# Cross-attention and a quantised feed-forward on one core: biases spread by TensorE, weight pieces loaded in series, shorter fillings

## The reference

```
x = x + xattn(layernorm(x), ctx, ctx)
    q, k, v = Wq x + bq, Wk ctx + bk, Wv ctx + bv      # 64 x 64, over the axis of 64
    per head h of 8 (64 columns): softmax(q_h k_h^T / 8) v_h ; then Wo . + bo
x = x + (silu(n @ G) * (n @ U)) @ W   with n = layernorm(x), G, U: 512 x 1792, W: 1792 x 512
    G = (gate_w - gate_z) * gate_s   per group of 128 rows, U and W likewise
```

## Time and profile before

| | |
|---|---|
| runs | 442.44, 443.42, 445.05 us; median 443.42 |
| the profiled execution | 441.19 us, of it 439.4 in the span of the instructions |
| first gate/up product | 51.65 us after the start of the span |
| busy | TensorE 94%, VectorE 75%, ScalarE 76%, GpSimd 62% |

### The profile page before, as it was taken

How to read it: one execution, slowest core, us unless ns; L and a number is a source line. 1 busy time by engine, 2 the same in 40 slices (tenths; PEclk the granted TensorE clock), 3 DMA queues, 4 the chain that set the end, 5 groups by cost and what they waited for, 6 DMA issues and landing times.

```text
span 439.4 us, 10920 instructions
## 1 busy us (share of the span) xinstructions
PE 414.5 (94%) x4318; PEld 325.2 (74%) x4318; DVE 328.9 (75%) x576; ACT 332.0 (76%) x542; POOL 270.6 (62%) x269
## 2 busy tenths in 40 slices
PE   7598898999997999999999999999999999999994
PEld 6476756777764777777877777687877888888872
DVE  4866647899779876879787876978887667677676
ACT  2236799889766978777868878777978998988970
POOL 4444696999597656655746656654666555555561
PEclk9989999999999999999999999999999999999999
DMA  7996261976652000000210000000010000001003
GB/s 195 362 326 199 75 207 57 331 244 217 207 185 66 25 1 27 1 27 0 75 51 24 1 1 25 3 25 25 0 50 2 0 2 0 24 25 48 2 1 95
DMA packets 26917, 35.52 MB, mean 81 GB/s; under 512 B 1962, under 2 KB 18514, under 8 KB 26866
## 3 DMA queue, kind: packets, MB, share of 16 engines
q1 hardware_dynamic: 26354, 34.69, 24.1%
q0 software_dynamic: 192, 0.07, 0.4%
q10 hardware_dynamic: 320, 0.07, 0.1%
HBM read 30.63 MB, written 4.19 MB: 79 GB/s over the span
## 4 chain that ended last, share of the span: by engine, by line
PE 72%; DVE 8%; issue 8%; ACT 6%; POOL 3%; DMA 1%; SPq 1%; POOLq 0%; DVEq 0%; ACTq 0%
PE banks L754 20%; PE banks L756 18%; PE banks L767 10%; PE banks L768 9%; PE banks L652 3%; ACT banks L554 2%; DVE yT L989 2%; PE banks L692 2%; PE banks L681 2%; PE banks L670 2%; PE banks L785 2%; PE banks L662 2%; DMA x_sb<-in_x 1%; DVE st L878 1%; POOL wgu_in L410 1%
## 5 line engine op out<-in xcount | busy, mean ns | idle before, releaser
L554 ACT ACTIVATE banks<-banks,ratio 128x512 f32<-128x512 f32 x336 | 208.0, 665 | 35.2 <-PE banks L756 25.6
L989 DVE SCALAR_TENSOR_TENSOR yT<-banks,sd,yT 128x512 f32<-128x512 f32 x208 | 154.1, 747 | 48.7 <-PE banks L768 48.1
L754 PE MATMUL banks<-xT,wgu 128*128 128x512 f32 x448 | 182.5, 407 | 4.7 <-DVE t_sb L974 3.4
L756 PE MATMUL banks<-xT,wgu 128*128 128x512 f32 x448 | 175.1, 391 | 0.0
L417 POOL TENSOR_TENSOR t_sb<-t_sb,u_sb 128x512 f32<-128x512 f32 x56 | 72.7, 1298 | 64.9 <-DVE t_sb L974 64.7
L754 PEld LDWEIGHTS banks<-xT,wgu 128*128 128x128 f32 x448 | 84.1, 188 | 27.5 <-issue 3.5
L756 PEld LDWEIGHTS banks<-xT,wgu 128*128 128x128 f32 x448 | 84.3, 188 | 15.1
L767 PE MATMUL banks<-hr,wd 128*128 128x512 f32 x224 | 89.3, 399 | 4.5 <-DVE yT L989 2.7
L768 PE MATMUL banks<-hr,wd 128*128 128x512 f32 x224 | 87.5, 391 | 0.0
L430 POOL TENSOR_TENSOR hr<-t_sb,hr 128x512 fp32r<-128x512 f32 x56 | 72.6, 1297 | 5.1 <-ACT hr L576 0.7
L767 PEld LDWEIGHTS banks<-hr,wd 128*128 128x128 f32 x224 | 42.0, 188 | 19.6 <-DVE yT L989 9.9
(11 more groups left out here) (88 smaller groups left out, 398.3 us busy)
## 6 DMA issues: line engine op xcount, KB each, us to landing
x_sb<-in_x SPq DMA_DIRECT2D x16, 256.0 KB, 5.7
out<-x_sb SPq DMA_DIRECT2D x16, 256.0 KB, 2.1
wgu_in<-in_L_ffn_gate_w SPq DMA_DIRECT2D x7, 512.0 KB, 8.1
z_in<-in_L_ffn_gate_z SPq DMA_DIRECT2D x7, 512.0 KB, 5.1
wgu_in<-in_L_ffn_up_w SPq DMA_DIRECT2D x7, 512.0 KB, 5.5
z_in<-in_L_ffn_up_z SPq DMA_DIRECT2D x7, 512.0 KB, 5.1
wd_in<-in_L_ffn_down_w SPq DMA_DIRECT2D x7, 512.0 KB, 5.5
z_in<-in_L_ffn_down_z SPq DMA_DIRECT2D x7, 512.0 KB, 4.7
```

The lines of the kernel that those rows point to most:

```text
L554: act.activation(banks[:, bank, :], banks[:, bank, :], ACT.Copy, scale=ratio[:, m, g, it:it + 1]).then_inc(done[n % 2], 1)
L754: pe.matmul(banks[:, bank, :], w, xT[:, c % 2, 0, g, :], start=g == 0, stop=False, skip_group_check=True)
L756: pe.matmul(banks[:, bank, :], w, xT[:, c % 2, 1, g, :], start=False, stop=True, skip_group_check=True).then_inc(full[n % 2], 1)
L989: dve.scalar_tensor_tensor(y, bank, sd[:, it, b:b + 1], y, ALU.mult, ALU.add).then_inc(s_free, 1)
```

## The change

Five edits. (1) bq, bk, bv and bo are loaded as rows of one partition; TensorE spreads them by products with a row of ones (bq and bk over 128 partitions in one product, bv and bo into columns by four), and VectorE copies the results to `bqk` and `bvo`. TensorE waits for bq and bk ahead of `project(0)`. The waits for `s_bvo` of ScalarE and VectorE become waits for the copy (`s_wT` at 3). (2) SyncE loads x and ctx of tiles 0 and 1 and x of tile 2 ahead of the scales, and then pieces 0 to 3 in series: it waits for the piece to land, issues the zeros, and waits for them. x of tile 4 goes behind piece 2, ctx of tile 3 behind piece 1, ctx of tile 4 behind the zeros of piece 2. (3) A filling is now a plain product of up to four blocks of 128 columns, and there are 50 blocks where there were 140 transposes. The new loads of bq and bk are issued on ScalarE's queue, between those of Wq, Wk and of Wv, Wo. (4) In the front `rest_x(j-3)` stands behind `residual(j-1)`, a tile later than before, and `norm2(j-2)` behind `norm1(j+2)`; only the last of each keeps its place. (5) `by_vector` holds from piece 4 on: pieces 4 and 6 go to VectorE.

```diff
     def by_vector(k):
-        return k >= 8 and k % 2 == 0
+        return k >= EARLY and k % 2 == 0
...
+        b_row = xn2[0:1, 1, 2 * P:2 * P + 4 * D].rearrange("a (m o) -> a m o", m=4)
+        ones = xn2[0:1, 0, 2 * P:3 * P]
...
-            load_x(0)
-            load_ctx(0)
-            load_x(1)
+            for t in range(2):
+                load_x(t)
+                load_ctx(t)
+            load_x(2)
...
-            load_ctx(1)
-            load_x(2)
-            load_w(0)
-            load_zeros(0)
             load_ctx(2)
             load_x(3)
-            load_w(1)
-            load_zeros(1)
-            load_ctx(3)
-            load_x(PRE)
-            load_ctx(PRE)
-            for k in range(2, NP):
+
+            for k in range(EARLY):
                 load_w(k)
-                if k == 3:
-                    load_x(PRE + 1)
-                    load_ctx(PRE + 1)
+                if 1 <= k < 3:
+                    (load_ctx if k == 1 else load_x)(k + 2)
+                sync.wait_ge(s_w[k], 16)
+                load_zeros(k)
+                if k == 2:
+                    load_ctx(PRE)
+                wait_zeros(sync, k)
+            load_x(PRE + 1)
+            load_ctx(PRE + 1)
+            for k in range(EARLY, NP):
+                load_w(k)
                 if k in CTX_AT:
                     load_ctx(CTX_AT[k])
                 load_zeros(k)
...
-            for m, v in enumerate((bq, bk)):
-                pool.dma_start(bqk[:, m, :],
-                               v.rearrange("(a o) -> a o", a=1).partition_broadcast(P)).then_inc(s_bias, 16)
-            for h in range(2):
-                for m, v in enumerate((bv, bo)):
-                    pool.dma_start(bvo[h * D:(h + 1) * D, m:m + 1],
-                                   v.rearrange("(o a) -> o a", a=1)).then_inc(s_bvo, 16)
+            pool.memset(ones, 1.0).then_inc(s_id, 1)
+            for m, v in enumerate((bv, bo)):
+                pool.dma_start(b_row[:, 2 + m, :], v.rearrange("(a o) -> a o", a=1)).then_inc(s_bvo, 16)
...
             load(s_wsm, wraw[:, 0, :], Wq)
             load(s_wsm, wraw[:, 1, :], Wk)
+            for m, v in enumerate((bq, bk)):
+                load(s_bias, b_row[:, m, :], v.rearrange("(a o) -> a o", a=1))
...
                 if j + 2 <= PRE:
                     norm1(j + 2)
+                if j >= 2:
+                    norm2(j - 2)
...
-                if j >= 1:
+                if j == PRE - 1:
                     norm2(j - 1)
...
             def stir(n, bank=RING_BANK + 1):
 
-                for _ in range(n):
-                    pe.transpose(banks[:, bank, 3 * P:4 * P], ident[:, :], ident[:, :])
+                while n > 0:
+                    k = min(n, NC)
+                    pe.matmul(blocks(bank)[:, 0:k, :], ident[:, :], ident[:, :].unsqueeze(1).to_broadcast([P, k, P]),
+                              start=True, stop=True)
+                    n -= k
...
-            stir(16)
+            stir(8)
...
-            stir(6)
+            pe.wait_ge(s_id, 4)
+            pe.wait_ge(s_bias, 32)
+            pe.matmul(banks[:, 7, 0:2 * D], ones, b_row[:, 0:2, :], start=True, stop=True).then_inc(s_brow, 1)
+            stir(1)
             pe.wait_ge(s_wT, 1)
             project(0)
-            stir(12)
+            stir(5)
...
+            pe.wait_ge(s_bvo, 32)
+            for m in range(2):
+                for r in HALVES:
+                    mm = pe.matmul(banks[r, 7, 4 * D + m:4 * D + m + 1], b_row[:, 2 + m, :], ones[:, 0:1],
+                                   start=True, stop=True)
...
                 if j + 1 < PRE:
-                    stir(6)
+                    stir(1)
...
-                    stir(5)
+                    stir(1 if j < PRE - 1 else 2)
                     pe.wait_ge(s_x1, j)
...
-                stir(6)
+                stir(2)
                 pe.wait_ge(s_v, j + 1)
                 mix(j)
-                stir(5)
+                stir(2)
                 apply(j)
             turn_x(PRE - 2)
-            stir(22)
+            stir(10)
...
-            stir(7, U_BANK[1])
+            stir(3, U_BANK[1])
...
-            dve.wait_ge(s_bias, 32)
+            dve.wait_ge(s_brow, 1)
+            dve.tensor_copy(bqk[:, :, :].rearrange("p m o -> p (m o)"), banks[:, 7, 0:2 * D]).then_inc(s_bqk, 1)
+            dve.wait_ge(s_bqk, 1)
...
                     take_w(1)
+                    dve.tensor_copy(bvo[:, :], banks[:, 7, 4 * D:4 * D + 2]).then_inc(s_wT, 1)
+                    dve.wait_ge(s_wT, 3)
                 else:
                     residual(j - 1)
+                if j >= 3:
+                    rest_x(j - 3)
                 invert(j)
...
-                if j >= 2:
+                if j == PRE - 1:
                     rest_x(j - 2)
```

More of the change, by code:

```diff
@@ L212, in xattn_ffn @@
         s_dif, s_deqa, s_deqv = sem("s_dif"), sem("s_deqa"), sem("s_deqv")
-        s_tr, s_wT, s_prep, s_scl, s_low = (sem(n) for n in ("s_tr", "s_wT", "s_prep", "s_scl", "s_low"))
+        s_tr, s_wT, s_prep, s_scl, s_low, s_brow, s_bqk = (
+            sem(n) for n in ("s_tr", "s_wT", "s_prep", "s_scl", "s_low", "s_brow", "s_bqk"))
         s_st = [sem(f"s_st{m}") for m in range(2)]
@@ L489, in _ @@
             act.wait_ge(s_warm, 1)
-            act.activation(warm[:, :], warm[:, :], ACT.Exp)
+            act.activation(warm[:, 0:1], warm[:, 0:1], ACT.Exp)
             load(s_wsm, wraw[:, 0, :], Wq)
             load(s_wsm, wraw[:, 1, :], Wk)
+            for m, v in enumerate((bq, bk)):
+                load(s_bias, b_row[:, m, :], v.rearrange("(a o) -> a o", a=1))
             load(s_wsm2, wraw[:, 2, :], Wv)
@@ L579, in _ @@
             norm1(1)
-            act.wait_ge(s_bvo, 64)
             for j in range(PRE):
@@ L589, in _ @@
                     act.copy(sd[:, :, :].rearrange("p g c -> p (g c)"), banks[:, 4, ng:ng + NI * NC]).then_inc(s_scl, 1)
+                if j == 0:
+                    act.wait_ge(s_wT, 3)
                 take_v(j)
@@ L817, in _ @@
                 if j == 0:
-                    pe.wait_ge(s_wT, 2)
+                    pe.wait_ge(s_wT, 3)
                 else:
-                    stir(5)
+                    stir(1 if j < PRE - 1 else 2)
                     pe.wait_ge(s_x1, j)
@@ L999, in add_last @@
                 dve.tensor_tensor(y, blocks(unit_bank(("YB", b))), y, ALU.add).then_inc(s_free, 1)
-            dve.memset(warm[:, :], 0.0).then_inc(s_warm, 1)
+            dve.memset(warm[:, 0:1], 0.0).then_inc(s_warm, 1)
             stats(0, 0)
@@ L1031, in _ @@
                     prepare()
-                    dve.wait_ge(s_bvo, 64)
                 if j == 1:
```

## The result

The changed kernel takes 439.35 us (median of 9 executions, 437.89 to 441.97) against 444.97 (9, 442.44 to 446.59): ratio 0.9882, 95% interval 0.9854 to 0.991, so 1.2% or some 5.3 us faster (5.6 us between the two medians). I had said 436.2, a gain of 7.2. The median lies 3.2 above that: inside the range of 431 to 441.5, but above the 434 to 438.5 that I had called the forecast. Two timed executions, one of the kernel before (579.86 us) and one of a kernel in the experiments (573.82), took some 30% longer at a granted clock of 0.65 and are in no ratio.

What follows compares the result with a forecast made beforehand. It took the front to be a chain through all engines and ScalarE the bound from 51.65 to 69.10 us. Gains of 5.3 in the front and 1.9 from two pieces made 7.2, so 436.2 us on the 443.42 median, range 431 to 441.5.

Steps and rivals of the forecast that it cites:

- the sum: Whole kernel: -5.3 us in the front and -1.9 behind it make -7.2, so 436.2 us on the median.
- the landing of x4: Front: x of tile 4, loaded behind piece 2, lands at 25.7 us, with 3.3 us taken for a weight piece alone.
- the -1.9 of the two pieces: Behind the front: pieces 4 and 6 leave ScalarE, the bound; first down product 15.1 us behind first gate/up product, 17.0 before.
- Start: First 20 us: `rstd(0,0)` at 4.4, `project(0)` at 6.6 (7.60 before), `residual(0)` at 19.9 instead of 23.81.
- The new wait for x4: Front: VectorE comes to `stats(0,4)` at 23.0 and waits 2.7 us for x4; `most(2)` starts at 26.9, against 28.11.
- Pairs in series: Front loads: one weight piece and its zeros take 7.6 us, bounds 6.8 and 9.8; at 11.2 the gain is used up.
- Tiles 2 and 3: Front from `most(2)` on: `rest_x(0)` a tile later, `most(3)` at 32.8 (39.4), first gate/up product at 45.4, 6.2 us earlier.
- The half rate that I forecast before `score(3)`: Front: TensorE stands some 4 us, then 3.4 us of products at half rate cost about 1 us; 5.3 taken, not 6.2.
- Stops: Front: TensorE's two "issue" stops, 3.34 and 0.97 us, put down to code fetch behind data traffic, would cost nothing afterwards.
- stops remain: Rival, front: the refill is hidden, so the 4.3 us of stops stay; about 3 us less is won, 439; chance 0.1.
- The clock rival: Rival, tiles 1 to 3: short fillings may not keep 2.4 GHz, about 4 us, 440; 0.15 together with slow VectorE halves.
- The rule on transposes: Trainium skill's rule, cited on TensorE's fillings: transposes don't count as busy for the clock; would make the clock rival unlikely.

Runs made afterwards that it cites:

- x4_c4: Changed kernel with x of tile 4 loaded behind piece 1 and ctx of tile 4 behind piece 2: 439.56 us, ratio 0.9878 to the kernel before.
- before_again: The kernel before, unchanged, timed and profiled once more: 445.18 us against 446.36, ratio 0.9964; the profiled execution took 447.55.
- e3: Changed kernel with 12 blocks of filling at the start instead of 8: 441.19 us, ratio 0.9894 to the kernel before.
- after_again: The changed kernel, unchanged, timed and profiled once more: 440.88 us, ratio 0.9867 to the kernel before.
- u_order: Changed kernel with `rest_x` and `norm2` of the front in their old places: 440.15 us, ratio 0.9896 to the kernel before.
- u_fill: Changed kernel with the old fillings, 140 transposes in the old places: 439.61 us, ratio 0.9878 to the kernel before.
- u_series: Changed kernel without the waits for the loads of pieces 0 to 3, all issued at once: 441.5 us, ratio 0.9919 to the kernel before.
- e2: Changed kernel with x of tile 4 loaded behind piece 1 instead of piece 2: 439.81 us, ratio 0.9872 to the kernel before.
- x4_c4_z6: x4_c4 with piece 6's zeros also issued earlier, two input tiles behind them: 436.47 us, ratio 0.9772 to the kernel before.
- e1: The kernel before with edit 5 alone (pieces 4 and 6 on VectorE): 443.59 us, ratio 0.9958.

## Why the prediction was right, and where its steps were off

**In part by luck.** In the two profiles that the sum is about, the change gained 2.8 us of the 7.2: 2.4 of 5.3 in the front and 0.4 of 1.9 behind it. What brought the timed executions to 5.3 fits with starts of the kernel before that are mostly worse than the one I read, and the sum had no such term. Two steps failed: the landing of x4, and the -1.9 of the two pieces.

**Start: mis-sized, and measured against a lucky execution.** Forecast -1.0 at `project(0)` and -4 at `residual(0)` (19.9). In the profile it was +0.8 and -0.5: TensorE was at 1.2 GHz until 13.9 us, so its products and fillings took double. x4_c4, at full clock from 5.3, has my 19.9 within 0.2: the steps were right, the clock that they took for granted wasn't. The clock column of the profile doesn't show this, since it reads 1.00 before the first change on record (8.38 to 12.73 us stands under 1.00); the products' own durations tell the rate. Against an execution of before that is as unlucky as before_again the same start gains 3.3 us at `project(0)`. That fits with a difference of 5.3 between the timed executions and 2.8 between the profiles, but two profiles of the kernel before and one of its near copy don't prove it.

**The new wait for x4: its length right by luck, its place wrong.** 2.46 us against 2.7 forecast. But VectorE came to it at 26.6 and not at 23.0, and x4 landed at 29.05 and not at 25.7: two misses of some 3.5 us that cancel. The second is the step that failed. I took 3.3 us for w0, the price of a piece alone, and it took 6.0 with x3 and c2 in flight. The first piece with its zeros took 10.5 us and not 7.6, and x4 stands behind it in the series. So `most(2)` came 3.3 us late and the first gate/up product 2.9 behind the forecast of 46.35 (51.65 - 5.3). The late start didn't do this: in e3, with `residual(0)` at 21.32, x4 held `most(2)` at 29.33 and the first gate/up product came at 50.94. On an earlier start the wait is longer, 3.63 us in e3 and 4.78 in after_again, and with it TensorE is at half rate for 6.8 us and not for 3.4.

**Pairs in series: right but for the first.** Behind the 10.5 of the first they took 7.8, 7.7 and 7.6 us (forecast 7.6; 11.2 was where the change would have lost). In other profiles in series the second pair took up to 9.9 (u_fill).

**Tiles 2 and 3: the number right, its cause not shown.** From `most(2)` to the first gate/up product 19.05 us, forecast 18.5 with the clock whole; before 23.54, and 22.64 in before_again. I had put the gain down to the new places of `rest_x` and `norm2`. Undone (u_order), they cost 0.5 us of it at equal clock. What gives the rest wasn't tested. The half rate that I forecast before `score(3)` didn't come in this profile, where TensorE stands 1.64 us there; it came in five others, which stand 3.0 to 5.8 us.

**Two pieces: right at its place, not at the end.** First down product 15.04 us behind the first gate/up product (forecast 15.1). Then 1.4 us of the lead over the kernel before, -4.2 at 71 us, go by 113 (-2.8). By the trace ScalarE stands at piece 7:

```profile
70.25 1.05 ACT L549 CAST wd<-wd_in 128x1024 fp32r<-128x1024 int32 x1 [0.98 <-POOL wd_in L410]
```

for GpSimd's subtraction, which took 2.8 us there. This is read off and wasn't tested. So the whole -1.9 isn't in the end time. This is the second step that failed: of the -1.9 about -0.4 is left at the end in the profiled pair.

**Stops: right.** 4.3 us became 0.8 (none above 0.3 was forecast), with u_series as the counter-proof. On the Trainium skill, Runtime: NRT & Kernel Launch, section Instruction fetch mechanics: its "mostly hidden" doesn't hold here. In the crowd of before the refill cost 3.3 us in each of three executions. With the loads in series, and the 16 DMA engines 0.20 to 0.31 busy during the stop, a single one of 1.3 to 1.5 us still stood in e2, e3 and u_fill. So with less traffic the stops were shorter here, and not gone. The rival that built on the page (stops remain, 439) came near the measured time for another reason.

**The clock rival.** Short fillings didn't cost the clock (u_fill is the same). From 12 us on there are twelve stops or waits of TensorE of 2.1 to 5.8 us in the 14 profiles, five of them that for x4, and each has a stretch at 1.2 GHz beside it; x4_c4_z6, which has none above 1.5 us, is at full rate throughout. But the change's own stretch, from 24.1 on, comes behind a stop of 0.80 and a wait of 0.43 us, and e2's, from 17.8, behind a stop of 1.32. There the wait for x4 isn't the cause, and what is stays open. The rule on transposes isn't borne out. With 140 of them (u_fill) or none, full clock first came at 9.8 us and at 4.9 to 13.9, which decides nothing. But in e1 it came at 4.7 us, and from 1.52 to there TensorE had run nothing but the old fillings, which are transposes:

```profile
1.52 3.50 PE L785 MATMUL banks<-ident 128*128 128x128 f32 x16 [1.52 <-POOL power L374]
5.35 0.45 PE L792 MATMUL banks<-ident,xn 64*64 64x64 f32 x8 [0.33 <-DMA xn<-in_L_xattn_Wk]
```

What TensorE did ahead of the span isn't on record.

**What the sum lacked.** A late load moved, it didn't go: without the wait for x4 (e2) the time stays, because VectorE then waits 3.66 us for the zeros of piece 6, a job that this same change gave it. I had listed its four halves by their durations, and had zeros of piece 6 landing at 50.5; they landed at 55.6. With both cut down (x4_c4_z6) the kernel gains 9.9 us; in the same session the change gained 5.5.

## What to carry to other kernels

Where an engine is given work on loaded data, write the landing of that data beside the moment when the engine comes to it, for the whole queue and not only for the first late load; here the second wait grew as the first was cured (from 1.94 us to 3.66 and 4.65) and hid what the cure was worth. Profile the kernel before more than once before a sum rests on its start: two executions differed by 5.1 us at the first gate/up product. And loads in series cost nothing here that could be told, while TensorE's stops with them were 0.8 us and without them 5.6; in the time of the whole that was 0.4%, which isn't told from nothing either.

## What the runs showed that I hadn't expected

- The start varies by execution: TensorE's full rate first came between 4.7 and 17.8 us after the start in 14 profiles, and the same 256 KB load, issued at 1.65 us, took 4.6 or 8.7. What decides it stays open.
- In the change's profile, 512 KB in series land in 3.8 to 4.0 us, whether weights or zeros spread to the partitions, from the second piece on; in other profiles single ones took up to 5.7. Behind 40 us, with four pieces in flight, it was 9.4 and 10.5.
- How long TensorE stays at 1.2 GHz doesn't follow from the wait before it. The wait of 5.8 us (after_again) had 6.8 us beside it, the 3.3 us stop of before 3.4; but nearly the same stop in e1 (3.26) had 6.8, and a wait of 4.07 in u_fill had 3.4.
- In seven of the 14 profiles there was one more such stretch of 3.4 us, which began 135 to 141 us in; x4_c4_z6 had none. Around it e1 and x4_c4 lost 0.7 and 0.9 us against the profile of before.
